# Scaling half of three layer normalizations on ScalarE, and three moves of work around it

## The chip, the core and the metric

The kernel runs on one core of one Trainium2 chip. The metric is the device time of one execution, in microseconds (us). PE is the matrix engine (TensorE), DVE is VectorE, ACT is ScalarE, POOL is GpSimd, and SP issues most of the transfers. The five run their own instruction streams and meet at semaphores.

## What is computed

Two transformer-like layers on a token array `x` of 2048 tokens by 128 features, all in float32 accuracy:

```
x = x + attention(layernorm(x))            # 16 heads with a decay
x = x + experts(layernorm(x))              # 160 experts, top 8, and a shared one
x = x + memory(layernorm(x))               # a 128x128 matrix, updated chunk by chunk
x = x + experts2(layernorm(x))             # 8 experts, top 2
layernorm(x) = (x - mean(x)) / sqrt(var(x) + 1e-5)     # over the 128 features
```

## The kernel before

The 2048 tokens lie as 16 tiles of 128 tokens (partitions) by 128 features. Four tiles are a group, and there are four groups, which I count from one in the text and the code counts from zero (`g`). Each engine's program is written out by hand, in the order in which it executes; nothing is scheduled by a tool.

There are four normalizations, `norm(0)` to `norm(3)`. The change touches the last three. I call the stretches around them stage A (`norm(1)`, ahead of the 160 experts, about 318 to 355 us), stage B (`norm(2)`, ahead of the memory, 798 to 818 us) and stage C (`norm(3)`, ahead of the 8 experts, 889 to 918 us). In each of them a group goes through five steps, one after the other:

1. DVE adds the result of the block before to `x`, takes the statistics of four tiles (L1686) and aggregates them into mean and variance (L1689).
2. POOL computes `rstd`, that is (variance + eps) to the power -0.5, in two small instructions (L685, L686).
3. DVE writes `xn`, which is (x - mean) times rstd, in four instructions (L1698). On DVE this step of a group stands behind the statistics of the next group.
4. PE transposes the four tiles of `xn` into a PSUM bank (L1175).
5. ACT copies the bank to `xnT` (L874), on which the matrix products of the block work.

What follows a group's copy differs:

- Stage A: PE does the shared expert's first product (L1307), then the router's logits (L1292), then adds biases to a later group's bank (L1286) once that bank has been read. ACT copies the shared product and takes its sigmoid (L1015, L1016), then takes the sigmoid of the logits into `gates` (L1009), then writes `xh`, a rounded copy of `xnT` (L882). DVE picks the top eight experts of each token (L1808 to L1818, L1822). When the last shared activation is there, PE clears its accumulators (L1266), and then transposes the chosen weights (L1447, L1448), which ACT scales (L1043) and copies (L1029, L1030, L1035). With these the loop over the experts begins, at 355 us.
- Stage B: PE makes two rows of token scalars per group (L1533), then sums of `xn` by chunk (L1523, L1541). PE is kept busy by products that nobody reads, called spares (L1185). DVE prepares weights and sums for these (L1968, L1978), and ACT applies a sigmoid (L887), for which it loads a table.
- Stage C: DVE first adds the memory's result to all of `x`, four instructions (L2046), and then normalizes. PE makes the router's logits (L1589), and has spares between the groups (L1172), then goes on to the up projections of the second experts (L1464), and at last spreads the chosen weights (L1617) that DVE computes from the logits (L2058 to L2094). ACT writes `xh` and POOL writes `xl` (L856), the two parts of `xnT` that the up projections read.

## Time and profile before

| | us |
|---|---|
| median of 3 runs | 1058.62 |
| lowest and highest of them | 1057.59, 1058.99 |
| the profiled execution, its time | 1059.15 |
| the profiled execution, its span in the trace | 1057.4 |
| PE busy | 1008.4 (95%) |
| DVE busy | 816.8 (77%) |
| ACT busy | 795.7 (75%) |
| POOL busy | 233.0 (22%) |

The profile shows the profiled execution alone. A row of its timeline gives the start of an instruction or of a run of equal ones (x4), counted from the start of the span, its length, the engine and the source line, and in brackets how long the engine was idle ahead of it and what ended that. The mean granted clock of PE over the span is 0.987 of full speed.

### The profile page before, as it was taken

Reading aid. Unit: us, or ns where it says so; the run is one execution under the profiler, and the core shown is the slowest. Engines: PE = TensorE matmul, PEld = TensorE weight load, DVE = VectorE, ACT = ScalarE, POOL = GpSimd, SP = SyncE. Lnnn points to the kernel's source line nnn. Section 1 sums busy time; section 2 is a strip of 40 time slices with the busy share of each in tenths; the row PEclk is TensorE's granted clock in tenths of the full one; section 3 lists DMA queues with packets and bytes.
Section 4 is the critical chain, followed back from the end, with each engine's and each line's share of the span. In section 5 each row is a group of like instructions: output and inputs, shape, how many; then the busy total and the mean of one; then the engine's idle time right before and its main releaser. Section 6 shows DMA issues by size and latency. Waiting matters only on the chain.

```text
span 1057.4 us, 20303 instructions
## 1 busy us (share of the span) xinstructions
PE 1008.4 (95%) x5242; PEld 684.2 (65%) x5274; DVE 816.8 (77%) x1861; ACT 795.7 (75%) x1331; POOL 233.0 (22%) x359
## 2 busy tenths in 40 slices
PE   5799999999998999999999999999998998999997
PEld 3333333333335688888888888888875887888885
DVE  8644444444449799999999999999996888699997
ACT  5799999999985778788787878778773553655554
POOL 3777765554463000000000000000005112200000
PEclk9799999999999999999999999999999999899999
DMA  4477876777761587677776777777631000034321
GB/s 134 143 230 242 255 250 219 235 225 226 225 202 36 180 309 246 240 243 235 240 241 241 246 245 236 235 245 242 237 98 60 1 2 1 1 128 125 106 102 40
DMA packets 102991, 188.98 MB, mean 179 GB/s; under 512 B 11932, under 2 KB 56604, under 8 KB 102940
## 3 DMA queue, kind: packets, MB, share of 16 engines
q1 hardware_dynamic: 102756, 188.19, 54.8%
q8 instruction: 18, 0.29, 0.1%
q10 hardware_dynamic: 192, 0.30, 0.1%
q14 instruction: 25, 0.20, 0.1%
HBM read 152.46 MB, written 35.98 MB: 178 GB/s over the span
## 4 chain that ended last, share of the span: by engine, by line
PE 86%; DVE 5%; ACT 3%; DMA 2%; issue 2%; POOL 1%; SPq 1%; DVEq 0%; ACTq 0%; POOLq 0%
PE bank L1464 28%; PE bank L1477 16%; PE bank L1362 12%; PE bank L1471 8%; PE bank L1343 6%; PE bank L1346 5%; PE bank L1562 1%; PE bank L1373 1%; DVE xn L1698 1%; PE bank L1185 1%; DVE stats L1686 1%; DVE state L2036 1%; DMA c_rows<-fold 1%; PE bank L1572 1%; PE bank L1292 1%
## 5 line engine op out<-in xcount | busy, mean ns | idle before, releaser
L1464 PE MATMUL bank<-xh,w_parts 128*128 128x512 f32 x896 | 277.4, 391 | 0.9 <-DVEq L1936 0.9
L969 ACT ACTIVATE ring<-bank,minus_bound 128x1024 f32<-128x1024 f32 x256 | 263.0, 1118 | 13.8 <-PE bank L1346 8.8
L1069 ACT ACTIVATE bank<-bank 128x512 f32<-128x512 f32 x320 | 186.2, 582 | 88.7 <-PE bank L1464 88.7
L1950 DVE TENSOR_TENSOR bank<-bank,ring 128x512 f32<-128x512 f32 x320 | 223.8, 699 | 25.2 <-DMA ring<-c_rows 2.8
L1477 PE MATMUL bank<-hh,w_parts 128*128 128x512 f32 x772 | 237.9, 389 | 0.0
L1942 DVE TENSOR_TENSOR hl<-bank,hh 128x512 fp32r<-128x512 f32 x321 | 218.4, 680 | 0.1
L1842 DVE TENSOR_TENSOR bank<-bank,corner 128x128 f32<-128x128 f32 x256 | 76.4, 298 | 154.3 <-PE bank L1346 151.2
L1464 PEld LDWEIGHTS bank<-xh,w_parts 128*128 128x128 f32 x896 | 168.0, 189 | 37.5 <-DVEq L1936 1.7
L1063 ACT ACTIVATE hh<-bank 128x512 fp32r<-128x512 f32 x321 | 190.4, 593 | 0.8 <-DVE bank L1950 0.5
L1464 PE MATMUL bank<-xl,w_parts 128*128 128x512 f32 x448 | 174.8, 390 | 0.0
L1477 PEld LDWEIGHTS bank<-hh,w_parts 128*128 128x128 f32 x772 | 144.8, 188 | 30.6 <-ACT hh L1063 0.8
L1471 PE MATMUL bank<-hl,w_parts 128*128 128x512 f32 x387 | 151.8, 392 | 2.5 <-DVE hl L1942 2.3
L1362 PE MATMUL bank<-ring,v_cur 128*32 128x512 f32 x1024 | 137.6, 610 | 0.1
L1343 PEld LDWEIGHTS bank<-q_stack,k_stack 128*128 128x128 bf16 x320 | 30.5, 98 | 115.8 <-ACT ring L969 96.3
L832 POOL MEMSET q_stack<- 128x512 f32 x2 | 1.0, 530 | 466.2 <-PE bank L1471 466.2
L1343 PE MATMUL bank<-q_stack,k_stack 128*128 128x384 bf16 (+2 forms) x320 | 97.7, 322 | 1.8 <-issue 0.2
L1346 PE MATMUL bank<-q_stack,k_stack 128*128 128x512 bf16 (+3 forms) x352 | 94.0, 327 | 4.2 <-DMA k_stack<-k_parts 4.2
L1464 PEld LDWEIGHTS bank<-xl,w_parts 128*128 128x128 f32 x448 | 84.4, 188 | 17.8
L1471 PEld LDWEIGHTS bank<-hl,w_parts 128*128 128x128 f32 x387 | 72.6, 188 | 22.3 <-DVE hl L1942 6.1
L1146 ACT ACTIVATE q_stack<-bank 128x512 f32<-128x512 f32 x58 | 34.7, 598 | 51.7 <-PE bank L1464 49.8
L2111 DVE TENSOR_TENSOR q_stack<-big,ring 128x512 f32<-128x512 f32 x64 | 44.3, 693 | 11.4 <-ACTq L1126 3.0
L1362 PEld LDWEIGHTS bank<-ring,v_cur 128*32 128x32 f32 x1024 | 20.2, 108 | 48.6 <-ACT ring L969 39.9
(320 smaller groups left out, 1137.7 us busy)
## 6 DMA issues: line engine op xcount, KB each, us to landing
ring<-c_rows SPq DMA_DIRECT2D x173, 512.0 KB, 4.7
w_parts<-w_pairs SPq DMA_DIRECT2D x160, 128.0 KB, 2.9
w_pairs<-xh SPq DMA_DIRECT2D x16, 768.0 KB, 4.3
q_stack<-q_parts SPq DMA_DIRECT2D x63, 144.0 KB
k_stack<-k_parts SPq DMA_DIRECT2D x189, 48.0 KB
w_pairs<-xl SPq DMA_DIRECT2D x16, 512.0 KB, 3.0
big<-in_w_exp SPq DMA_DIRECT2D x16, 384.0 KB, 4.8
w_ffn_parts<-xl SPq DMA_DIRECT2D x16, 384.0 KB, 3.7
```

Of the source, the lines that this page charges most:

```text
L969: act.activation(ring[:, c % RING * S:(c % RING + 1) * S], wide[(m + c) % SB][:], ACT.Exp, bias=minus_bound[:]).then_inc(exp_done, 1)
L1063: act.activation(hh[(c - 1) % 2][:], hidden, ACT.Copy).then_inc(split, 1)
L1069: act.activation(bank(4 + c % ZB), bank(4 + c % ZB), ACT.Silu).then_inc(silu_ready, 1)
L1343: ins = pe.matmul(wide[(m + c) % SB][:, lo:mid], k_stack[0][u][:, keys], q_stack[1][u][:, lo:mid], start=True, stop=True)
L1346: ins = pe.matmul(wide[(m + c) % SB][:, mid:hi], k_stack[1][u][:, keys], q_stack[0][u][:, mid:hi], start=True, stop=True)
L1362: ins = pe.matmul(bank(6 + u)[at:at + 32, :], v_cur[u][:, done_step % QT, :], ring[:, at_ring + h * 512:at_ring + (h + 1) * 512], start=(d ...
L1464: ins = pe.matmul(out_, w[i], x_[j], start=start and k == 0, stop=stop and k == 2, skip_group_check=not start)
L1471: return pe.matmul(bank(done_step % G), w[0], hl[done_step % 2][:], start=False, stop=False, skip_group_check=True)
L1477: ins = pe.matmul(bank(done_step % G), part, hh[done_step % 2][:], start=opens and k == 0, stop=False, skip_group_check=True)
L1842: dve.tensor_tensor(tile, tile, corner[:], ALU.mult).then_inc(corner_done, 1)
L1942: dve.tensor_tensor(hl[(c - 1) % 2][:], hidden, hh[(c - 1) % 2][:].bitcast(F32), ALU.subtract).then_inc(split, 1)
L1950: dve.tensor_tensor(bank(4 + c % ZB), bank(4 + c % ZB), cb[u][:, g * GW:(g + 1) * GW], ALU.mult).then_inc(hid_ready, 1)
```

## The change

In `norm(1)` to `norm(3)` groups two and four are no longer scaled by DVE but by ACT. ACT's instruction multiplies by one value per token and adds one per token, so POOL makes a second one, `shift` = -mean times rstd, in two more small instructions for each such group. A new semaphore, `odd_ready`, tells PE that ACT has done a group. On ACT a group's four scaling instructions stand ahead of the copy of the group before it.

In stage A PE makes a group's logits ahead of its shared product, ACT takes them in the same order, and DVE's first small product for the shared expert stands behind the first group's choice. In stage B the table for the sigmoid is loaded ahead of the normalization. In stage C DVE adds the memory's result of a group just ahead of that group's statistics, and PE's spares are three behind each group's transposes, into a bank of their own, with the group's logits right behind them.

```diff
@@ POOL
+                    if k and g % 2:
+                        link.sign(pool.tensor_scalar(shift[:, ts], mv[:, ts, 0], -1.0, None, ALU.mult))
                     link(pool.tensor_scalar(rstd[:, ts], mv[:, ts, 1], EPS, None, ALU.add))
-                    pool.tensor_tensor(rstd[:, ts], rstd[:, ts], half[:, ts], ALU.pow).then_inc(rstd_ready, 1)
+                    ins = pool.tensor_tensor(rstd[:, ts], rstd[:, ts], half[:, ts], ALU.pow)
+                    if k and g % 2:
+                        link(ins)
+                        ins = pool.tensor_tensor(shift[:, ts], shift[:, ts], rstd[:, ts], ALU.mult)
+                    ins.then_inc(rstd_ready, 1)
@@ ACT, norm(k, follow)
-                for g in range(G):
-                    n = G * k + g
-                    act.wait_ge(xnT_psum, n + 1)
-                    cols = slice(g * GW, (g + 1) * GW)
-                    act.activation(xnT[:, cols], bank(n % 2), ACT.Copy).then_inc(xnT_ready, 1)
-                    if g:
-                        follow(g - 1)
+                for g in range(G + 1):
+                    if g < G and g % 2:
+                        act.wait_ge(rstd_ready, G * k + g + 1)
+                        for t in range(g * TPG, (g + 1) * TPG):
+                            ins = act.activation(xn[:, t, :], x[:, t, :], ACT.Identity, bias=shift[:, t:t + 1], scale=rstd[:, t:t + 1])
+                        ins.then_inc(odd_ready, 1)
+                    if g >= 1:
+                        n = G * k + g - 1
+                        act.wait_ge(xnT_psum, n + 1)
+                        cols = slice((g - 1) * GW, g * GW)
+                        act.activation(xnT[:, cols], bank(n % 2), ACT.Copy).then_inc(xnT_ready, 1)
+                    if g >= 2:
+                        follow(g - 2)
@@ ACT, take_group(g)
+                take_logits(g)
                 act.wait_ge(shared_psum, g + 1)
...
-                take_logits(g)
                 high_x(g, 1)
@@ ACT, ahead of norm(2)
+            act.activation(early_table[:], half[:, 0:1], ACT.Sigmoid)
             norm(2, token_gates)
@@ PE, norm(k, read_group, spares)
-                    for _ in range(spares if g else 0):
-                        pe.matmul(bank(n % 2), hh[0][:, 0:P], hh[0][:], start=True, stop=True)
-                    pe.wait_ge(xn_ready, n + 1)
+                    if k == 0:
+                        pe.wait_ge(xn_ready, g + 1)
+                    elif g % 2:
+                        pe.wait_ge(odd_ready, G // 2 * (k - 1) + g // 2 + 1)
+                    else:
+                        pe.wait_ge(xn_ready, G + G // 2 * (k - 1) + g // 2 + 1)
...
-                    if read_group and g:
+                    if spares:
+                        for _ in range(spares):
+                            pe.matmul(bank(7), hh[0][:, 0:P], hh[0][:], start=True, stop=True)
+                        read_group(g)
+                    elif read_group and g:
                         read_group(g - 1)
@@ PE, tokens_of(g)
+                    router_logits(g)
                     shared_hidden(g)
-                    router_logits(g)
@@ PE
-            norm(3, router_logits2, 4)
+            norm(3, router_logits2, 3)
@@ DVE, norm(k, make_x)
-                    if g >= 1:
+                    if g >= 1 and (k == 0 or g % 2):
@@ DVE, choose_experts
-                shared_product(0)
                 for g in range(G):
+                    if g == 1:
+                        shared_product(0)
@@ DVE, ahead of norm(3)
-            for g in range(G):
+            def add_memory(g):
...
-            norm(3)
+            norm(3, add_memory)
```

Two places in the order of instructions matter most. The first is ACT in stage A, from the first copy on. `big` is where the gates go, `k_stack` and `q_stack` hold the shared product and its sigmoid, and L1043 is the scaling of the chosen weights. Before:

```order
L874 ACTIVATE xnT<-bank 128x512 x2
L1015 ACTIVATE k_stack<-bank 64x512
L1016 ACTIVATE q_stack<-bank 64x512
L1009 ACTIVATE big<-bank 128x640
L882 ACTIVATE xh<-xnT 128x512
L874 ACTIVATE xnT<-bank 128x512
L1015 ACTIVATE k_stack<-bank 64x512
L1016 ACTIVATE q_stack<-bank 64x512
L1009 ACTIVATE big<-bank 128x640
L882 ACTIVATE xh<-xnT 128x512
```

The same place of the changed kernel:

```order
L882 ACTIVATE xn<-x,shift,rstd 128x128 x4
L888 ACTIVATE xnT<-bank 128x512 x2
L1022 ACTIVATE big<-bank 128x640
L1029 ACTIVATE k_stack<-bank 64x512
L1030 ACTIVATE q_stack<-bank 64x512
L896 ACTIVATE xh<-xnT 128x512
L882 ACTIVATE xn<-x,shift,rstd 128x128 x4
L888 ACTIVATE xnT<-bank 128x512
L1022 ACTIVATE big<-bank 128x640
L1029 ACTIVATE k_stack<-bank 64x512
L1030 ACTIVATE q_stack<-bank 64x512
```

The scaling of group two has come ahead of the first copy, that of group four ahead of the copy of group three and behind all of group one's work, and each group's gates are ahead of its shared product.

The second is PE in stage C. `w_gate` are the logits, `hh` the spares, `ident,xn` the transposes, and the last row is the first up projection. Before, from the second group's transposes on:

```order
L1175 MATMUL bank<-ident,xn 128x128 x4
L1589 MATMUL bank<-w_gate,xnT 128x8 x4
L1172 MATMUL bank<-hh 128x512 x4
L1175 MATMUL bank<-ident,xn 128x128 x4
L1589 MATMUL bank<-w_gate,xnT 128x8 x4
L1172 MATMUL bank<-hh 128x512 x4
L1175 MATMUL bank<-ident,xn 128x128 x4
L1589 MATMUL bank<-w_gate,xnT 128x8 x8
L1464 MATMUL bank<-xh,w_parts 128x512 x2
```

The changed kernel, from the second group's transposes on:

```order
L1192 MATMUL bank<-ident,xn 128x128 x4
L1196 MATMUL bank<-hh 128x512 x3
L1610 MATMUL bank<-w_gate,xnT 128x8 x4
L1192 MATMUL bank<-ident,xn 128x128 x4
L1196 MATMUL bank<-hh 128x512 x3
L1610 MATMUL bank<-w_gate,xnT 128x8 x4
L1192 MATMUL bank<-ident,xn 128x128 x4
L1196 MATMUL bank<-hh 128x512 x3
L1610 MATMUL bank<-w_gate,xnT 128x8 x4
L1485 MATMUL bank<-xh,w_parts 128x512 x2
```

The logits of a group used to stand behind the transposes of the next one. Now they stand behind its own, with three spares between, so one group's logits are left behind the last transposes where there were two.

## Rows read from the trace of the kernel before

**Rows 1.** The page, chain that ended last, shares by engine.

```profile
PE 86%; DVE 5%; ACT 3%; DMA 2%; issue 2%; POOL 1%; SPq 1%; DVEq 0%; ACTq 0%; POOLq 0%
```

**Rows 2.** Windows of 2 us, stage A: length, PE busy, granted clock, DMA.

```profile
328.00:330.00 2.00, 2.00 (x8) 0.50 0.00 0
```

**Rows 3.** Timeline, PE, stage A: start, us, line, operands, idle before.

```profile
326.21 0.66 PE L1175 MATMUL bank<-ident,xn 128*128 128x128 f32 x4 [2.34 <-DVE xn L1698]
...
336.00 0.60 PE L1175 MATMUL bank<-ident,xn 128*128 128x128 f32 x4
...
338.82 1.07 PE L1307 MATMUL bank<-xnT,w_shared 128*64 128x512 f32 x2
...
341.16 1.19 PE L1266 MATMUL bank<-hh 128*128 128x512 f32 x4
...
346.38 0.30 PE L1447 MATMUL bank<-ident,ring 128*128 128x128 f32 x1 [0.72 <-issue]
```

**Rows 4.** Timeline, ACT, stage A.

```profile
340.52 0.58 ACT L1016 ACTIVATE k_stack<-bank 64x512 f32<-64x512 f32 x1
...
342.33 2.65 ACT L1043 ACTIVATE ring<-ring,top_inv 128x160 f32<-128x160 f32 x8
```

**Rows 5.** Timeline, DVE, stage A, and the PE row that takes its last result.

```profile
325.04 1.11 DVE L1698 TENSOR_SCALAR xn<-x,mv,rstd 128x128 f32<-128x128 f32 x4
...
326.07 0.68 DVE L1792 TENSOR_TENSOR x<-x,bank 128x512 f32<-128x512 f32 x1
...
328.04 1.11 DVE L1698 TENSOR_SCALAR xn<-x,mv,rstd 128x128 f32<-128x128 f32 x4
...
346.97 0.83 DVE L1822 TENSOR_TENSOR ring<-ring,top_inv 128x640 f32<-128x640 f32 x1
...
350.83 0.33 PE L1447 MATMUL bank<-ident,ring 128*128 128x128 f32 x1 [0.25 <-ACT fold L1030]
```

**Rows 6.** Timeline, POOL, stage A.

```profile
322.15 0.32 POOL L685 TENSOR_SCALAR rstd<-mv 128x4 f32<-128x4 f32 x1 [0.23 <-DVE mv L1689]
...
322.55 1.04 POOL L686 TENSOR_TENSOR rstd<-rstd,half 128x4 f32<-128x4 f32 x1
```

**Rows 7.** Lines, ACT, stage A: busy us, mean ns of one, idle before.

```profile
L1043 ACT ACTIVATE ring<-ring,top_inv 128x160 f32<-128x160 f32 x12 | 4.0, 414 | 0.0
```

**Rows 8.** Timeline, PE and POOL, stage B.

```profile
809.87 0.63 PE L1175 MATMUL bank<-ident,xn 128*128 128x128 f32 x4 [1.02 <-DVE xn L1698]
...
811.85 0.66 PE L1175 MATMUL bank<-ident,xn 128*128 128x128 f32 x4
...
818.35 0.63 PE L1541 MATMUL bank<-tok_sum,ident 2*128 2x32 f32 x4
...
808.73 0.31 POOL L685 TENSOR_SCALAR rstd<-mv 128x4 f32<-128x4 f32 x1 [1.57 <-DVE mv L1689]
```

**Rows 9.** Timeline, DVE and POOL, stage C.

```profile
889.31 2.48 DVE L2046 TENSOR_TENSOR x<-x,bank 128x512 f32<-128x512 f32 x4 [0.81 <-PE bank L1580]
...
900.75 3.01 DVE L1698 TENSOR_SCALAR xn<-x,mv,rstd 128x128 f32<-128x128 f32 x4 [0.54 <-POOL rstd L686]
...
900.62 1.28 POOL L856 TENSOR_TENSOR xl<-xnT,xh 128x512 fp32r<-128x512 f32 x1
```

**Rows 10.** Timeline, PE, stage C.

```profile
900.76 0.96 PE L1589 MATMUL bank<-w_gate,xnT 128*128 128x8 f32 x8
...
904.45 3.42 PE L1589 MATMUL bank<-w_gate,xnT 128*128 128x8 f32 x16
...
907.72 1.20 PE L1464 MATMUL bank<-xh,w_parts 128*128 128x512 f32 x2
...
911.15 0.39 PE L1464 MATMUL bank<-xl,w_parts 128*128 128x512 f32 x1
...
918.03 3.73 PE L1617 MATMUL bank<-ident,combine 128*128 128x128 f32 x32
```

**Rows 11.** Windows of 1 us, PE, stage C.

```profile
905.00:906.00 1.00, 1.00 (x6) 0.50 0.00 0
```

More of the change, by code:

```diff
@@ L113, in build @@
         ident = sb("ident", [P, P])
+        shift = sb("shift", [P, NT])
         half = sb("half", [P, NT])
@@ L304, in build @@
         xn_ready = sem("xn_ready")
+        odd_ready = sem("odd_ready")
         xnT_psum = sem("xnT_psum")
@@ L1176, in norm @@
                     ins.then_inc(xnT_psum, 1)
-                    if read_group and g:
+                    if spares:
[3 more added lines that the diff above has]
+                    elif read_group and g:
                         read_group(g - 1)
-                if read_group:
+                if read_group and not spares:
                     read_group(G - 1)
@@ L1312, in tokens_of @@
                     pe.wait_ge(xnT_ready, G + g + 1)
+                    router_logits(g)
                     shared_hidden(g)
-                    router_logits(g)
+                    if g < G - 2:
+                        pe.wait_ge(gate_ready, g + 1)
+                        router_biases(g + 2)
                 norm(1, tokens_of)
```

3 lines of the change are left out of this document (removed).

## The prediction

> **What bounds the kernel now.** I read the page first, then the chain that ended last, then the three stretches around the changed normalizations engine by engine in the timeline, and last the granted clock there. PE holds 86% of the chain [rows 1], and that is the loops over heads, experts and chunks, which the change leaves alone. Whatever it gives or takes, it does in stages A, B and C, 70 us together. In each of them the question is which engine's work ends last, since DVE, which loses work here, need not be that engine.
>
> Stage A. PE transposes group two at 326.21 after 2.34 us of waiting for `xn` [rows 3]. It then runs without a long gap to the last group's shared product at 338.82. ACT's last shared sigmoid starts at 340.52 and takes 0.58 [rows 4]. PE's clearing at 341.16 waits for it, and from there PE goes through nine more products and a branch to the first transposes of chosen weights at 346.38 [rows 3]. ACT copies them and is busy up to the expert loop at 355. DVE's choice of experts ends at 346.97 + 0.83 = 347.8, and PE takes it at 350.83, after a wait for ACT's copy and not for DVE [rows 5]. So DVE has 3.0 us to spare there. What bounds stage A is the way to the last shared sigmoid. In the middle of it PE has half its clock: 0.50 is granted in 328 to 330 [rows 2], that is 1.2 of 2.4 GHz, after the wait of 2.34 us.
>
> Stage B. PE waits for DVE once more at 809.87, for group three, transposes group four at 811.85, and then works through to the sums at 818.35 [rows 8]. Group four's transposes carry the rest with them.
>
> Stage C. DVE adds for 2.48 us before it takes the first statistics. Its scaling of group four takes 3.01 where the others take 1.11, while POOL's `xl` runs from 900.62 on [rows 9, 5]. PE stands idle, loses half its clock (0.50 granted at 905 to 906 [rows 11]), makes the last 16 logits instructions in 3.42 us where 8 took 0.96 at the full clock, starts the up projections at 907.72 and the spreading at 918.03 [rows 10]. Of the 36 products of the up projections 28 come from 911.15 to about 917.6, 0.23 us each, and the first eight took 907.72 to 911.15, 0.43 each [rows 10].
>
> The Trainium skill (page "SBUF — State Buffer", section "SBUF: two separate sides") has DVE and GpSimd take one shared pair of ports as a lock for a whole instruction, and ScalarE never wait for it. By that rule the 1.9 us of DVE's long scaling go away when ACT does it; the trace agrees so far as the two instructions lie side by side.
>
> **What the change costs and gives, part by part.**
>
> POOL. An odd group (two and four) gets two more small instructions. `shift` goes ahead and costs about 0.3, by the 0.32 of L685; the product behind the power costs 0.2 to 0.3 and a wait for it. A group takes from 322.15 to 323.6 [rows 6]; it will take 2.0 instead of 1.45.
>
> ACT's price for one tile is not in the trace. The nearest is L1043, one value per token, 160 columns: eight of them in 2.65, or 0.33 each when they overlap [rows 4], and 0.414 for one alone [rows 7]. Four cost 1.3 at the low end and 1.66 laid end to end. I take 1.6 since a second value per token is read. DVE's four cost 1.03 from start to next start, 325.04 to 326.07 [rows 5]. So a scaling is dearer on ACT, and what it may gain is place.
>
> The Trainium skill (page "ScalarE: Activation LUTs", section "What ACT_TABLE_LOAD costs") gives 186 ns and 0.833 ns per column, 93 ns more for each value per token, and 93 ns of overlap. By that page four would cost an estimated 1.64. The sum would be the same by it as by the upper end above.
>
> DVE. A group's turn is 3.00 from 325.04 to 328.04 [rows 5], of which 1.97 are left for an odd group.
>
> Stage A, with these. Group two: POOL is done at 322.15 + 2.0 = 324.1, ACT at 325.5 to 325.8, against 326.15 before (325.04 + 1.11). PE begins its transposes 0.4 to 0.7 earlier. Group one's gates come next, now ahead of its shared product, and are ready near 329, not 331.5. But on ACT the scaling of group four stands behind all of group one's shared work and ahead of the copy of group three. I followed the four queues with the durations of the trace, and leave the half clock where it was. ACT comes free at 331.9, scales until 333.4, copies group three until 333.9 and gives the gates of group two at 334.5. PE transposes group four at 335.0, which is 1.0 ahead of 336.00 [rows 3]. Then the new order takes it back. Before, the way from there to the end of the last sigmoid was 341.10 - 336.00 = 5.1 us. Now the last shared product stands behind the last logits, a step of 1.3, and it ends at 341.4. That is +0.3 at the dear price of ACT, and -0.6 in the expert loop's start at the cheap one; with the full clock all along it is +0.45 and -0.1. I take 0.0, bounds -0.6 and +0.6. DVE's choice begins 2 us earlier and ends 1 to 2 us earlier, which only adds to its spare time.
>
> Stage B. POOL began on group four at 808.73 [rows 8]; with one scaling less ahead of it (1.03) it begins at 807.7. POOL is done 2.0 later, with the latency at 809.6, and ACT at 811.3, with group four's transposes behind it, against 811.85 [rows 8]. -0.5, and -0.8 by the cheap ACT. Group three comes 1.0 earlier but PE has to wait for four all the same. The table load moves from a place where nobody waited to another; 0.
>
> Stage C. The first statistics begin 1.8 earlier, since three of the four adds come behind them; group four's end at 889.3 + 4 x 1.97 + 1.03 = 898.2, POOL is done at 900.2, ACT's scaling at 902.2 to 903.1, against 903.76 before (900.75 + 3.01). PE's last transposes come at 902.3 to 904, and behind them stand three spares and one group's logits instead of two. The logits are all there at 906.1 with the full clock, against 907.87. The up projections then take 36 x 0.23 = 8.3 and can't use it all, since ACT must load two tables before it takes the first banks (a new wait of 1 us for PE). The spreading starts at 916.4: -1.6. But PE now waits at group one's logits for a copy that stands behind group two's scaling, from 895.9 to 897.5. If that brings half the clock for one stretch, the same path gives 918.06: 0.0. Three of four parts to the first: -1.2.
>
> The sum is 0.0 - 0.5 - 1.2 = -1.7 on the profiled execution's 1059.15 (its span of 1057.4 and 1.75 around it), 1057.4. The profiled execution is 0.5 above the median of 1058.62 and above all three runs shown, as the place of its half-clock stretches can make it. Against the median the forecast is -1.2, or -0.1%. Less than 0.2%, 2.1 us, can hardly be told from no change here.
>
> **The rivals.**
>
> *The clock stays full* (faster). If PE's waits are short enough in A and C, the half-clock stretches go. Before they cost 1.7 in A (the same queues followed at the full clock bring ACT's last copy to 353.1, not 354.9). In C the spreading comes at 915.3 to 916.4. For it: PE's waits in A and C get shorter in sum, and the first in A shrinks from 2.34. Against it: it shrinks by only 0.5, and the spares are no more than before. -1.7 -0.5 -2.7 = -4.9: 1054.2.
>
> *ACT in PE's way* (slower). In C each copy that PE waits for is queued on ACT behind a scaling, with group one's logits at once behind. If PE's clock is halved already near 898 and again later, logits, transposes and spares up to 906 run at double length and the spreading comes at 921, +3.1. With 0.0 in A and no gain in B, it is 1062.2. It decides when PE idles for over 3 us in all between 895 and 901. For it: PE no longer has a group's transposes to do while it waits. Against it: the three spares are then just ahead of the wait.
>
> *Nothing arrives* (same). A gains nothing by its order, B's sums wait for POOL's second root, which is 0.5 later in its queue than without `shift`, and C falls to the second of its two cases: 1058.7 to 1059.8.
>
> **How the numbers follow.** Forecast 0.50, between 1056.5 and 1058.7; nothing arrives 0.17; the full clock 0.22; ACT in the way 0.11. The forecast's own bounds are A -0.6 to +0.6, B -0.8 to -0.3, C -1.6 to 0. The range of 1054.6 to 1060.6 reaches over the middle of the fast rival and up to near the slow one. Faster by over 0.2% is 0.22, slower 0.11, and the rest, 0.67, is within it.
>
> **What would show it.** ACT's four scalings take 1.3 to 1.7 from the first to the last. In A the gates of group one are taken near 329, group four is transposed near 335.0, and the last shared sigmoid still ends near 341.4; DVE's choice ends by 346.5 and PE still takes it after ACT. In B group four's transposes start 0.5 earlier against the stage's first add than before. In C no scaling of DVE is longer than 1.2, and the spreading comes 1.6 earlier than before, counted from the memory's first add at 889.31. The clock's rows tell which case has come. Wrong would be the forecast if ACT's scaling took over 2 us, if an added table load stood before it, or if the half-clock stretches move to other places than in the trace of before.

## The result

| | kernel before | changed kernel |
|---|---|---|
| median of 20 runs each, alternating on one chip | 1058.32 | 1061.78 |
| lowest and highest of them | 1053.09, 1061.79 | 1057.66, 1065.76 |
| the profiled execution, its span | 1057.4 | 1059.1 |
| mean granted TensorE clock over that span | 0.987 | 0.984 |

The ratio is 1.0034 with a 95% interval of 1.0023 to 1.0045: slower, by 3.6 us. The forecast was 1057.4, range 1054.6 to 1060.6, so the time is outside the range and on the side that had a chance of 0.11.

PE's share of the chain that ended last went from 86% [rows 1] to 87%:

```profile
PE 87%; DVE 4%; ACT 3%; DMA 2%; issue 1%; POOL 1%; SPq 1%; DVEq 0%; ACTq 0%; POOLq 0%
```

**Stage C of the changed kernel.** PE's timeline (start, length, engine, line, operands, idle ahead), from the first group's transposes to the first up projection:

```profile
894.34 0.61 PE L1192 MATMUL bank<-ident,xn 128*128 128x128 f32 x4
894.71 0.96 PE L1196 MATMUL bank<-hh 128*128 128x512 f32 x3
897.57 1.06 PE L1610 MATMUL bank<-w_gate,xnT 128*128 128x8 f32 x8 [1.90 <-ACT xnT L888]
898.48 0.64 PE L1192 MATMUL bank<-ident,xn 128*128 128x128 f32 x4
898.87 1.33 PE L1196 MATMUL bank<-hh 128*128 128x512 f32 x3
900.00 1.71 PE L1610 MATMUL bank<-w_gate,xnT 128*128 128x8 f32 x8
...
905.29 1.09 PE L1192 MATMUL bank<-ident,xn 128*128 128x128 f32 x4
906.04 1.63 PE L1196 MATMUL bank<-hh 128*128 128x512 f32 x3
907.46 1.71 PE L1610 MATMUL bank<-w_gate,xnT 128*128 128x8 f32 x8
909.03 1.20 PE L1485 MATMUL bank<-xh,w_parts 128*128 128x512 f32 x2
```

ACT and DVE over the same stretch:

```profile
895.39 1.65 ACT L882 ACTIVATE xn<-x,shift,rstd 128x128 f32<-128x128 f32 x4 [7.48 <-POOL shift L693]
896.94 0.57 ACT L888 ACTIVATE xnT<-bank 128x512 f32<-128x512 f32 x1
...
900.37 1.65 ACT L882 ACTIVATE xn<-x,shift,rstd 128x128 f32<-128x128 f32 x4
...
889.10 0.69 DVE L2069 TENSOR_TENSOR x<-x,bank 128x512 f32<-128x512 f32 x1 [0.81 <-PE bank L1601]
...
898.04 1.12 DVE L1719 TENSOR_SCALAR xn<-x,mv,rstd 128x128 f32<-128x128 f32 x4
```

Windows of the same stage (length, PE busy, granted clock):

```profile
894.00:898.00 4.00, 2.10 (x14) 1.00 0.00 0
...
902.00:907.00 5.00, 5.00 (x21) 0.50 0.00 0
907.00:912.00 5.00, 5.00 (x17) 0.50 0.00 0
912.00:913.00 1.00, 1.00 (x4) 0.56 0.00 0
```

What the edit was drawn to do on DVE and ACT, it does. No scaling of DVE is longer than 1.12, where group four's took 3.01 [rows 9], and ACT's four take 1.65. ACT is done with group four at 902.02, 12.9 us after the first addition, against 14.45 before (900.75 + 3.01 - 889.31). But PE reaches group four's transposes only at 905.29, 16.2 after that addition, where before it was 14.5. It did not wait for ACT there; the work ahead of those transposes ran at half the clock. Eight logits take 1.06 at 897.57 and 1.71 from 900.00 on. The clock is 0.50 until 912, so the first nine of the 36 up projections run at half clock too. Over the stage 6.83 us of clock are lost (the sum of one less the granted clock over windows of 1 us), before 3.42. That the half-clock stretches move to other places was one of the prediction's own signs of being wrong.

**Stages A and B.** Times in brackets are counted from the stage's first addition on DVE. In A, group two is transposed at (8.08), before (8.14); group four at (17.10), before (17.93); and the clearing stands at (23.24), before (23.09). The expert loop starts at (36.27), before (37.02); 0.72 of that is the gap named "issue" of [rows 3], which the changed kernel's two traces don't have. In B the sums come at (20.00) with one half-clock stretch, before (19.89) without. The loop's first coefficients come by DMA, and DVE waits for them:

```profile
355.50 0.70 DVE L1972 TENSOR_TENSOR bank<-bank,ring 128x512 f32<-128x512 f32 x1 [2.21 <-DMA ring<-c_rows]
...
365.50 0.70 DVE L1972 TENSOR_TENSOR bank<-bank,ring 128x512 f32<-128x512 f32 x1 [2.33 <-DMA ring<-c_rows]
```

Before, these waits were 1.84 and 0.93. The expert loop starts with the first up projection on PE. From there to stage B's first addition it is 445.4 us, before 443.4.

### The profile page after: what moved, and what is told of

The parts are those of the page before. It is cut to its first block, busy times and chain, and to the rows that moved or that the text cites. A ratio compares the mean times of both kernels' runs of the same rounds, so it can differ in the third digit from the quotient of the medians.

```text
span 1059.1 us, 20346 instructions
## 1 busy us (share of the span) xinstructions
PE 1011.8 (96%) x5274; PEld 686.9 (65%) x5274; DVE 807.4 (76%) x1837; ACT 804.4 (76%) x1356; POOL 236.0 (22%) x371
## 4 chain that ended last, share of the span: by engine, by line
PE 87%; DVE 4%; ACT 3%; DMA 2%; issue 1%; POOL 1%; SPq 1%; DVEq 0%; ACTq 0%; POOLq 0%
PE bank L1485 28%; PE bank L1498 16%; PE bank L1383 12%; PE bank L1492 8%; PE bank L1367 6%; PE bank L1364 6%; PE bank L1583 1%; PE bank L1394 1%; PE bank L1206 1%; DVE state L2058 1%; DMA c_rows<-fold 1%; PE bank L1192 1%; PE bank L1593 1%; ACT xn L882 1%; DMA ring<-c_rows 1%
## 5 line engine op out<-in xcount | busy, mean ns | idle before, releaser
L983 ACT ACTIVATE ring<-bank,minus_bound 128x1024 f32<-128x1024 f32 x256 | 262.5, 1122 | 11.8 <-PE bank L1367 6.6
L1972 DVE TENSOR_TENSOR bank<-bank,ring 128x512 f32<-128x512 f32 x320 | 223.9, 700 | 27.1 <-DMA ring<-c_rows 4.5
L1367 PE MATMUL bank<-q_stack,k_stack 128*128 128x512 bf16 (+3 forms) x384 | 98.7, 330 | 3.7 <-DMA k_stack<-k_parts 3.6
L1485 PEld LDWEIGHTS bank<-xl,w_parts 128*128 128x128 f32 x448 | 84.5, 189 | 17.7
L2133 DVE TENSOR_TENSOR q_stack<-big,ring 128x512 f32<-128x512 f32 x64 | 44.3, 692 | 11.3 <-ACTq L1140 2.9
```

The source lines that it names most:

```text
L983: act.activation(ring[:, c % RING * S:(c % RING + 1) * S], wide[(m + c) % SB][:], ACT.Exp, bias=minus_bound[:]).then_inc(exp_done, 1)
L1367: ins = pe.matmul(wide[(m + c) % SB][:, mid:hi], k_stack[1][u][:, keys], q_stack[0][u][:, mid:hi], start=True, stop=True)
L1485: ins = pe.matmul(out_, w[i], x_[j], start=start and k == 0, stop=stop and k == 2, skip_group_check=not start)
L1972: dve.tensor_tensor(bank(4 + c % ZB), bank(4 + c % ZB), cb[u][:, g * GW:(g + 1) * GW], ALU.mult).then_inc(hid_ready, 1)
```

## How the experiments are read

A single trace turned out to be a weak witness here. Which stretches have half the clock differs between two executions of one kernel, and the time with it: the kernel before ran from 1052 to 1062 us. So each kernel ran 12 times (the changed kernel a second time, as after_again, 6 times), with runs of the kernel before beside it, and with each run comes its mean granted clock. The **clock lost** of a run is its span times one less that clock. Over 384 runs of all kernels, each counted from its own kernel's mean, a microsecond of lost clock goes with 0.56 us of time (correlation 0.81). This slope is taken within kernels; where it is used below to turn a difference between two kernels into time, the result is an estimate. The mean loss of a kernel is thus a second measurement beside its time. Drawing again from the runs at random (a bootstrap) gives the difference of two such means an interval of about 2 us to each side, so that the differences of 5 to 6 below are clear, those of 2 to 3 just so or not, and those under 2 are not.

The runs beside one another were on one chip, but the batches of experiments were on four different ones, and the median of the kernel before went from 1056.75 to 1058.32 between batches. The changed kernel itself came out at 1.0034 in one batch and 1.0064 in another. So a kernel is best compared with the kernel before beside it, and differences of 1 us between kernels of different batches say little. Three single runs of two experiments (c_old_order 1068 and 2536 us, all_old_order_more 1666 us) are left out of the means of the clock. The ratio of c_old_order still has the run of 1068 us in it; the mean of its ten others is 1056.7, against 1058.0 for the kernel before beside it, which is 0.9988.

| run | median us | ratio to before (95%) | clock lost, mean us | the same of before, beside it |
|---|---|---|---|---|
| the changed kernel | 1061.78 | 1.0034 (1.0023, 1.0045) | 17.5 | |
| after_again | 1062.23 | 1.0064 (1.0040, 1.0087) | 17.7 | 11.3 |
| only_a | 1058.04 | 1.0018 (1.0003, 1.0032) | 11.6 | 11.3 |
| only_b | 1056.82 | 0.9999 (0.9984, 1.0014) | 10.2 | 11.3 |
| only_c | 1060.11 | 1.0038 (1.0019, 1.0058) | 17.7 | 11.3 |
| adds_only | 1057.74 | 0.9992 (0.9978, 1.0005) | 12.2 | 12.6 |
| c_dve | 1059.25 | 1.0008 (0.9994, 1.0022) | 16.0 | 12.6 |
| c_filled | 1058.12 | 1.0003 (0.9990, 1.0016) | 10.4 | 12.6 |
| c_old_order | 1056.55 | 1.0001 (0.9978, 1.0025) | 11.6 | 12.6 |
| new_order_only | 1059.79 | 1.0027 (1.0008, 1.0046) | 17.0 | 11.4 |
| c_four_spares | 1058.91 | 1.0018 (0.9998, 1.0038) | 13.1 | 11.4 |
| b_and_c_old_order | 1056.20 | 0.9988 (0.9972, 1.0003) | 11.6 | 11.4 |
| a_scalings_only | 1057.96 | 1.0007 (0.9989, 1.0024) | 12.2 | 11.4 |
| old_order_three | 1058.29 | 1.0017 (1.0000, 1.0033) | 14.4 | 11.8 |
| new_order_four | 1058.56 | 1.0011 (0.9997, 1.0026) | 12.2 | 11.8 |
| b_and_c_more_spares | 1055.76 | 0.9989 (0.9974, 1.0003) | 11.0 | 11.8 |
| a_logits_only | 1056.58 | 0.9990 (0.9975, 1.0006) | 11.3 | 11.8 |
| logits_b_and_c | 1054.16 | 0.9961 (0.9946, 0.9977) | 8.4 | 12.0 |
| all_old_order_more | 1057.40 | 0.9993 (0.9978, 1.0008) | 10.8 | 12.0 |

"The stage's time" below is what the traces show from the stage's first addition on DVE; in stage C up to the spreading, which is 28.7 us before and 30.5 in the changed kernel.

## The experiments

**Which stage.** Each takes one stage's part of the change alone into the kernel before (ACT's scalings, and what else of the change stands in that stage; the cut below shows the scalings alone), and the last is the changed kernel once more. In code, the changed kernel's `if k and g % 2` becomes:

```diff
+ON_ACT = (1,)      # only_a; (2,) in only_b, (3,) in only_c
-                    if k and g % 2:
+                    if k in ON_ACT and g % 2:
```

> The part of stage A alone (ACT scales groups two and four there, logits ahead of the shared product; the rest as before). Theory 1, that the loss is made in stage C by ACT's scaling in PE's way and by half-clock stretches: within 1 us of before, as the last shared sigmoid ends 0.1 to 0.3 later only. Rival, that stage A loses by the order on ACT and by transfers at the start of the expert loop: +1.5 to +3 us.

> The part of stage B alone (ACT scales there, table loaded ahead). Theory 1: -0.5 to +0.7 us, the latter where a half-clock stretch falls on the token scalars. Rival: all three stages lose about alike, +1 us or more here.

> The part of stage C alone (adds between the statistics, ACT scales, three spares and a group's own logits behind each group's transposes). Theory 1: nearly the whole loss, +2.5 to +4 us, with half clock granted for 6 us or more between 897 and 914. Rival: within 1 us of before.

> The changed kernel once more beside its parts, for a second trace and for the sum. All theories: +2.4 to +4.8 us. If the parts are independent, the three others add up to this within 1.5 us.

Stage C's part alone gives the whole loss of clock, 17.7 against 11.3 us, and a ratio of 1.0038. Stage A's part costs something too, 1.0018, with the clock lost about the same; stage B's none. The three parts add up to 3.4 us of median, and after_again measured 5.0 over the kernel before beside it, just above what was expected of it. It ran only six times, and the changed kernel's first 20 runs stood 3.5 above theirs. The changed kernel's stage C came out alike three times: the spreading at 30.5, 30.7 and, with C's part alone, 30.5, each time with 6.83 lost.

**Which part of stage C.** My theory was that ACT's scaling ahead of the copy made the 1.90 us wait, and the wait halved the clock. Four runs took it apart. Each cut shows what matters of the edit.

```diff
@@ adds_only: the kernel before, and only this
-            for g in range(G):
+            def add_memory(g):
-            norm(3)
+            norm(3, add_memory)
@@ c_dve: the changed kernel, and this
+ON_ACT = (1, 2)
@@ c_filled: the changed kernel, and this
-                        for _ in range(spares):
+                        for _ in range(spares[g]):
-            norm(3, router_logits2, 3)
+            norm(3, router_logits2, (11, 6, 6, 6))
@@ c_old_order: the changed kernel, and this
-                        for _ in range(spares):
-                            pe.matmul(bank(7), hh[0][:, 0:P], hh[0][:], start=True, stop=True)
-                        read_group(g)
+                    for _ in range(spares if g else 0):        # ahead of the transposes, as before
+                        pe.matmul(bank(n % 2), hh[0][:, 0:P], hh[0][:], start=True, stop=True)
...
+                    if read_group and g:
+                        read_group(g - 1)
-            norm(3, router_logits2, 3)
+            norm(3, router_logits2, 4)
```

> The kernel before with one part of the change alone: in stage C the three later additions of the memory stand between the statistics; DVE keeps all four scalings and PE its old order. Theory 1 (the loss of stage C comes from ACT's scalings and PE's new order, not from the additions): the statistics of the first group come 1.8 us earlier, and at worst the same half-clock stretch stays, so the spreading is due at 27.0 to 28.7 us from the stage's first addition (28.7 before) and the time is 0 to 1.6 us under the kernel before. Theory 2 (the additions between the statistics hold DVE up for the later groups and so open the gaps on PE): the spreading comes at 29.5 or later, with more than 3.4 us of clock lost in the stage, and the time is at or above the kernel before.

> The changed kernel with one thing undone: in stage C DVE scales groups two and four again, with the additions between the statistics and PE's new order as in the changed kernel. Theory 1 (ACT's scaling of group two stands ahead of its copy of group one, PE waits 1.9 us for that copy and then has half its clock): without the scaling on ACT PE's copy of group one comes near 5.2 + 0.7 us in the stage instead of 8.3, no wait of over 1 us is there, 3.4 us of clock or less is lost in stage C, and the spreading is due by 28.7; 1.5 to 2 us under the changed kernel. Theory 2 (the loss is PE's new order, with the transposes of the next group no longer ahead of the logits, so that PE has nothing to do while it waits for DVE and POOL): the clock lost stays near 6.8 us and the spreading at 30 or later; within 0.5 us of the changed kernel.

> The changed kernel with more of PE's spare products in stage C: 11, 6, 6 and 6 behind the four groups' transposes instead of 3 each, nothing else. Theory 1 (the loss in stage C is the half clock that follows PE's waits): the spares lie in the waits, the clock stays at 2.4 GHz for all or nearly all of the stage (lost 0 to 1.7 us against 6.8), and the spreading is due at 26 to 28 us from the first addition against 30.5; 2 to 4 us under the changed kernel, so at or under the kernel before. Theory 2 (the loss is the queue on ACT itself, the copies behind the scalings and table loads): the clock may be full, but the spreading still comes at 30 or later and the time is that of the changed kernel or above it.

> The changed kernel with PE's old order in the normalizations: four spares ahead of each group's transposes in stage C, and a group's logits behind the transposes of the next group; ACT still scales groups two and four. Theory 1 (ACT's scaling ahead of the copies is the cause): the last transposes still wait for ACT, PE's gaps are as long as in the changed kernel, the clock lost stays at 5 us or more and the spreading at 29.5 or later; within 1 us of the changed kernel. Theory 2 (PE's new order is the cause): clock lost 3.4 us or less, the spreading by 28.7, 1.5 us or more under the changed kernel.

The additions are harmless, and by themselves worth nothing: with the full clock throughout the spreading stands at 27.2 in adds_only, and at 27.1 in only_b, whose stage C is that of the kernel before. With ACT's scalings undone in C (c_dve) the 1.90 us wait is gone, as theory 1 said, and yet the clock is lost all the same: 6.82 in the trace, 16.0 in the mean of the runs. PE's timeline and windows of c_dve:

```profile
896.45 1.06 PE L1609 MATMUL bank<-w_gate,xnT 128*128 128x8 f32 x8
898.04 0.66 PE L1191 MATMUL bank<-ident,xn 128*128 128x128 f32 x4 [0.54 <-DVE xn L1718]
898.46 0.95 PE L1195 MATMUL bank<-hh 128*128 128x512 f32 x3
899.39 1.35 PE L1609 MATMUL bank<-w_gate,xnT 128*128 128x8 f32 x8
901.14 1.08 PE L1191 MATMUL bank<-ident,xn 128*128 128x128 f32 x4 [0.40 <-DVE xn L1718]
...
895.00:899.00 4.00, 3.46 (x23) 1.00 0.00 0
...
901.00:912.00 11.00, 10.86 (x38) 0.50 0.00 0
```

Ahead of the fall PE waited 0.54 us, and the half clock came. In the kernel before it waited 1.09 and 0.62 there and had the full clock until the third wait. So the theory that the wait for ACT's copy takes the clock falls. The time did not go by theory 2 alone, though: c_dve's median is 1059.25, 2.5 under the changed kernel, where theory 2 had them within 0.5, and its spreading came 0.7 earlier (29.8). With PE's new order ACT's scalings in C thus seem to cost some time beside the clock; only_c and new_order_only, which differ by the scalings and the additions, are only 0.3 us of median apart, so this stays open.

The run with ACT's scalings and PE's old order settles what loses the clock: 11.6 us lost, 5.9 fewer than in the changed kernel, and a median of 1056.55 beside 1057.94 of the kernel before. In its trace the spreading is at 25.7. A single trace says little here, too: a later version, b_and_c_old_order, has the same instructions in stage C, lost 6.82 us there in its trace and spread at 29.9; over its 12 runs it, too, lost 11.6. PE in c_old_order, then in b_and_c_old_order, from the second group's transposes on:

```profile
896.29 0.66 PE L1193 MATMUL bank<-ident,xn 128*128 128x128 f32 x4 [1.19 <-ACT xn L883]
...
901.26 0.66 PE L1193 MATMUL bank<-ident,xn 128*128 128x128 f32 x4 [0.16 <-ACT xn L883]
901.75 2.04 PE L1607 MATMUL bank<-w_gate,xnT 128*128 128x8 f32 x16
```

```profile
894.15 0.65 PE L1193 MATMUL bank<-ident,xn 128*128 128x128 f32 x4 [1.19 <-ACT xn L883]
...
901.06 1.05 PE L1193 MATMUL bank<-ident,xn 128*128 128x128 f32 x4
901.91 3.42 PE L1607 MATMUL bank<-w_gate,xnT 128*128 128x8 f32 x16
```

The extra spares (c_filled) take the loss away too, 10.4, and the spreading stands at 27.7 without any half clock: 2 us later than with the old order; with 29 spares where there were 12, PE transposes group four at (14.74) and not at (12.96).

**The order, or the number of spares.** The new order has one spare fewer at each group, though 12 in all as before (four times three, not three times four).

```diff
@@ new_order_only, new_order_four: the kernel before, and this, with 3 or 4
-                    for _ in range(spares if g else 0):
-                        pe.matmul(bank(n % 2), hh[0][:, 0:P], hh[0][:], start=True, stop=True)
...
-                    if read_group and g:
-                        read_group(g - 1)
+                    for _ in range(spares):
+                        pe.matmul(bank(7), hh[0][:, 0:P], hh[0][:], start=True, stop=True)
+                    read_group(g)
@@ c_four_spares: the changed kernel, and this
-            norm(3, router_logits2, 3)
+            norm(3, router_logits2, (4, 4, 4, 4))
@@ old_order_three: the kernel before, and this
-            norm(3, router_logits2, 4)
+            norm(3, router_logits2, 3)
```

> The kernel before with one thing alone: PE's new order in stage C (three spares behind each group's transposes and then that group's own logits, instead of four spares ahead of the transposes of groups two to four and the logits of the group before behind them). DVE keeps all scalings, the additions all stand ahead. Theory 1 (the order is what costs the clock in stage C, as the run with the order undone and the one with ACT's scalings undone suggest): the half clock begins within a few us of the first logits and holds to the up projections, 5 to 7 us of clock are lost in the stage, the spreading comes 2 to 4 us later than in the kernel before, and the time is 1.5 to 3.5 us over it. Theory 2 (the order costs only together with the additions between or with ACT's scalings): clock lost in stage C 3.4 us or less, the spreading at 27 to 28.8, within 1 us of the kernel before.

> The changed kernel with four spare products behind each group's transposes in stage C instead of three, nothing else. Theory 1 (the place of the spares and of the logits decides, not the one spare): the clock is lost as in the changed kernel, 5 us or more in stage C, and the spreading stands at 30 or later; time within 1 us of it. Theory 2 (the one spare fewer per group is what tips it): clock lost 3.4 us or less, the spreading at 26.5 to 28.5, and 2 us or more under the changed kernel.

> The kernel before with three spares ahead of the transposes of groups two to four in stage C instead of four, so 9 in all instead of 12, and nothing else. Over the runs of a kernel the clock lost (span times one less the granted clock) has been 10.6 to 12.7 us in the middle for the kernel before and 16 to 18 with PE's new order and three spares. Theory 1 (the number of spares near each group is what tips it): 15 us or more lost in the mean of the runs, and 1.5 to 3 us over the kernel before. Theory 2 (the place is what tips it: logits, wait and transposes in a row without the next group's transposes between them): 11 to 13 us lost and within 1 us of the kernel before.

> PE's new order alone, as in an earlier run, but with four spares behind each group's transposes instead of three, 16 in all. Theory 1 (the number of spares near each group): 11 to 13 us of clock lost in the mean of the runs, against 17.0 with three, and within 1 us of the kernel before. Theory 2 (the place): 16 us or more lost and 2 to 3 us over the kernel before.

The new order with three spares, and nothing else of the change, loses 5.6 us of clock more than the kernel before and is at 1.0027. A fourth spare takes nearly all of that back: 12.2 against 11.8 lost. In the changed kernel it takes most of it, 13.1 against 17.5. And three spares in the old order lose 2.6 more than four. So the number counts: a fourth spare is worth 2.6 us of clock in the old place and 4.8 in the new one. The place counts with three spares, 2.6 in the old place against 5.6 in the new one, which the 12 runs of each barely tell apart, and hardly with four (none against 0.4). In time the same four kernels stand at 1.0017, 1.0027, 1.0011 and, for the kernel before, 1, with intervals that overlap, so the ranking rests on the clock. Three things go together in the new place and were not separated: the spares stand behind the transposes and not ahead of them, the group's own logits stand between them and the next wait, and they write another bank. The trace of new_order_only shows where, the rows that answer to [rows 10]:

```profile
903.28 1.09 PE L1190 MATMUL bank<-ident,xn 128*128 128x128 f32 x4 [1.23 <-DVE xn L1717]
904.02 1.63 PE L1194 MATMUL bank<-hh 128*128 128x512 f32 x3
905.44 1.71 PE L1608 MATMUL bank<-w_gate,xnT 128*128 128x8 f32 x8
907.01 1.20 PE L1483 MATMUL bank<-xh,w_parts 128*128 128x512 f32 x2
...
900.00:902.00 2.00, 2.00 (x14) 1.00 0.00 0
902.00:904.00 2.00, 0.77 (x5) 0.52 0.00 0
```

Here the clock falls in the wait for group four. With only one group's logits behind group four's transposes, the up projections start at 907.01, 18.4 after the first addition, as before; the half clock then stays for more of them and the spreading comes at 29.6. c_four_spares shows how little one trace says: its own had 5.12 us lost in stage C and the spreading at 31.1, later than any other, while its 12 runs lost 4.4 us less than the changed kernel. Its median lies between the two kernels, as neither theory had it.

**Stage A's two halves, and a faster version.**

```diff
@@ a_scalings_only: the kernel before, and ACT's scalings in norm(1)
+ON_ACT = (1,)
@@ a_logits_only: the kernel before, and the logits first on PE, ACT and DVE (ACT's part shown)
+                take_logits(g)
                 act.wait_ge(shared_psum, g + 1)
...
-                take_logits(g)
@@ b_and_c_old_order: scalings in B and C, additions between, stage A as before
+ON_ACT = (2, 3)
+            norm(3, add_memory)
@@ b_and_c_more_spares: the same, and spares (0, 7, 4, 5) in the old place
@@ logits_b_and_c: the same, and the logits first in stage A
@@ all_old_order_more: the same, and ON_ACT = (1, 2, 3)
```

> The kernel before with the scalings of groups two and four on ACT in stages B and C, and the additions between the statistics, but PE's old order in stage C and nothing changed in stage A. Theory 1 (stage C gains once PE keeps its old order, and stage A's part of the change costs 1 to 2 us up to stage B by whatever cause): the spreading at 25.7 to 26.5 from the stage's first addition, B's sums 0.2 to 0.5 earlier, and 2 to 3 us under the kernel before: the fastest of all. Theory 2 (stage A's part costs nothing): the same time as the changed kernel with the old order in C alone, within 0.7 us.

> The kernel before with one thing alone: ACT scales groups two and four in stage A, in front of its copies of groups one and three, while the logits stay behind the shared product. Theory 1 (the shift of the last shared product behind the last logits is what stage A pays): the transposes come as early as in the changed kernel, the clearing 1 us before it, at 22.2 or so from the stage's first addition, and the time is at or 0.5 to 1 us under the kernel before. Theory 2 (ACT's scalings ahead of the copies are what it pays): the transposes of group four no earlier than in the kernel before, the clearing at 23.1 or later and the time at or 1 to 2 us above the kernel before.

> The run with the scalings on ACT in stages B and C, the additions between and PE's old order, nothing of stage A, which measured 1056.20 and lost 11.6 us of clock in the mean; now with 7, 4 and 5 spares ahead of the transposes of groups two, three and four instead of 4 each. If the clock in stage C hangs on the spares, 8 to 10 us are lost in the mean and the time is 1 to 2 us under that run, 2 to 3 under the kernel before. If the added spares delay the transposes as much as the clock gives back, it is the same as that run.

> The kernel before with one thing alone: in stage A the router's logits stand ahead of the shared product on PE, ACT and DVE, and DVE keeps all scalings. Theory 1 (this order is what makes stage A dearer, by the last shared product behind the last logits): the clearing 0.5 to 1 us later than in the kernel before with the same clock, and 0.5 to 1.5 us over it. Theory 2 (ACT's scalings are): no later than the kernel before, within 0.5 us of it. Beside that, the seventh product with the experts' coefficients on DVE starts 10.2 to 11.3 us after the first up projection in the kernels with the old stage A, and 11.3 to 13.4 in those with the new one; where it stands at 12 or more here, the order of the logits is tied to it, and where at 11.3 or less, it is not.

> The version with ACT's scalings in stages B and C, the additions between, PE's old order and 7, 4 and 5 spares, plus the logits ahead of the shared product in stage A; DVE keeps the scalings of stage A. If the parts add up (that version measured 0.9989 and the logits alone 0.999), this one comes at 0.998, 1.5 to 3 us under the kernel before, the first to be faster than it beyond doubt. If the two gains were each chance, it is within 1 us of the kernel before.

> The changed kernel with one thing undone, PE's order in stage C (four spares ahead of the transposes and the logits a group later), and with 7, 4 and 5 spares; so the version beside it plus ACT's scalings in stage A. If ACT's scalings in stage A cost 0.5 to 1 us, as the runs of A's halves suggest (1.0007 with them alone, 0.999 with the logits alone), this is 0.5 to 1.5 us over the version beside it, and 3 to 5 us under the changed kernel with 10 to 12 us of clock lost. If they cost nothing, the two are equal within 0.5 us.

ACT's scalings are what stage A pays, by most of these runs. logits_b_and_c and all_old_order_more differ by them alone, and stand at 0.9961 and 0.9993: 3.2 us of median (by a bootstrap of the means 1.7 to 4.7), of which an estimated 1.3 is clock (2.4 more lost, at 0.56). That is more than the 0.5 to 1.5 that was expected. Alone they cost 1.0 (a_scalings_only). Two other kernels that differ by the whole of stage A's part, c_old_order and b_and_c_old_order, are within 0.4 us, as theory 2 of the latter had it, so the size is uncertain. The traces show the place. In the changed kernel ACT scales group four ahead of group three's copy and group two's gates, and PE waits for those gates (ACT first, then PE):

```profile
330.43 1.64 ACT L882 ACTIVATE xn<-x,shift,rstd 128x128 f32<-128x128 f32 x4
331.96 0.58 ACT L888 ACTIVATE xnT<-bank 128x512 f32<-128x512 f32 x1
332.44 0.69 ACT L1022 ACTIVATE big<-bank 128x640 f32<-128x640 f32 x1
...
333.18 0.57 PE L1307 MATMUL bank<-bias_rows,ones_r 128*128 128x320 f32 x2 [1.11 <-ACT big L1022]
333.59 0.60 PE L1192 MATMUL bank<-ident,xn 128*128 128x128 f32 x4
```

With the logits first and DVE scaling (a_logits_only) PE has no wait between its rows there:

```profile
329.59 1.07 PE L1321 MATMUL bank<-xnT,w_shared 128*64 128x512 f32 x2
330.59 0.56 PE L1303 MATMUL bank<-bias_rows,ones_r 128*128 128x320 f32 x2
330.99 0.60 PE L1192 MATMUL bank<-ident,xn 128*128 128x128 f32 x4
```

Group four is transposed at (15.83) and the clearing stands at (21.97), against (17.93) and (23.09) before and (17.10) and (23.24) in the changed kernel, all with 1.70 us of clock lost in the stage. So with that loss the logits first give 1.1 us, and ACT's scalings take 1.3. With the full clock throughout stage A the clearing is at (21.51) in the old stage A (only_b) and at (21.81) in the changed one (c_old_order): 0.3 late and not 0.15.

logits_b_and_c beats both kernels: 1054.16, 0.9961 of the kernel before (0.9946 to 0.9977) and 7.6 us of median under the changed one. The gain is twice what the two parts had measured (0.9989 and 0.9990), so part of it may be chance. Its stage C, PE again:

```profile
894.14 1.84 PE L1187 MATMUL bank<-hh 128*128 128x512 f32 x7
896.52 0.66 PE L1193 MATMUL bank<-ident,xn 128*128 128x128 f32 x4 [0.53 <-ACT xn L883]
...
901.51 0.66 PE L1193 MATMUL bank<-ident,xn 128*128 128x128 f32 x4
902.00 2.04 PE L1607 MATMUL bank<-w_gate,xnT 128*128 128x8 f32 x16
...
914.20 3.73 PE L1635 MATMUL bank<-ident,combine 128*128 128x128 f32 x32
...
900.00:905.00 5.00, 5.00 (x33) 1.00 0.00 0
```

The spreading comes 25.7 us after the first addition. Of the five versions with PE's old order and ACT's scalings in C, the three with 7, 4 and 5 spares had no half clock in stage C in their traces and lost 11.0, 8.4 and 10.8 us over the whole program in the mean; the two with four each lost 1.71 and 6.82 in stage C in their traces and 11.6 in the mean. That leans to more spares, and doesn't prove them.

## Why the prediction was wrong

**Durations of the parts**: right. ACT's four scalings measured 1.65 (taken 1.6, bounds 1.3 to 1.7). The 1.64 that the prediction estimated from the Trainium skill (page "ScalarE: Activation LUTs", section "What ACT_TABLE_LOAD costs") agrees. A POOL group with `shift` takes 2.2 with the latencies between (2.0). The long scaling of DVE is gone, and in c_dve, where DVE scales group four again, it takes 1.99 beside one `xl` of POOL (901.40 to 902.68), against 3.01 beside two. That fits the rule of the Trainium skill (page "SBUF — State Buffer", section "SBUF: two separate sides"). The stage did not get shorter for it.

**Stage A, 0.0**: right as a sum (the clearing at +0.15), wrong in its parts. The prediction let ACT's scalings give the gain and wrote that the new order "takes it back". Measured it is the other way: the order alone gives 1.1, the scalings alone come to (24.23), 1.1 late with more clock lost (3.41 in the stage against 1.70), and group two's transposes come 0.06 earlier and not 0.4 to 0.7. ACT started them at (6.38), 0.3 later than drawn, and was dearer than the cheap end by as much.

**Stage B, -0.5**: right in sign, too large. Without a half-clock stretch the sums come at (19.71) to (19.74), -0.15 to -0.2. POOL begins at the predicted time, but its chain and ACT's end 0.3 later than drawn. only_b's ratio, 0.9999, has room for either.

**Stage C, -1.2**: this step failed. "Three of four parts to the first" was the first of two cases, the full clock, and the other was one stretch of half clock. Both left out what the spares do for the clock: the sum for the new order counted "three spares and one group's logits instead of two" as length only, and the sentence against the fast rival, that "the spares are no more than before", put no price on having three at each wait instead of four. With the old order the gain that the step describes is there where the clock holds: 25.7 against 28.7, -3.0, of which about 1.6 is clock (with the full clock the kernel before's stage C takes 27.1). With the new order and three spares it is +1.8.

**The rival "ACT in PE's way"** named the outcome, 1062.2, with a chance of 0.11, and had the clock halved near 898 for +3.1 in C. The changed kernel's clock fell near 899, but the mechanism was wrong, so that the number comes out near 1061.78 is mostly luck: C gave +1.8, and the rest came from elsewhere. It was to come when PE idles over 3 us between 895 and 901; PE idled 1.9 there in the changed kernel and 0.9 in c_dve between 895 and 902, and the clock fell in both. Its sentence against, "the three spares are then just ahead of the wait", was the point: three were not enough in that place. The loss of clock in C is the order with its spares (new_order_only 1.0027), and ACT's scalings in C cost nothing that shows once the order is the old one.

**The bill** is an estimate. 17.5 against some 12 us of lost clock, 5.5 at 0.56, is 3.1 of the 3.6 us. ACT's scalings in stage A take about 2 beside the clock and the logits there give about 1; stage C's additions and scalings give 1.4 at the full clock. That leaves about 1 us open, which is within what the runs can tell. A candidate is the wait for the first coefficients: from the loop's start to stage B it is 442.8 to 444.0 us in the ten traces in which at most one stage is changed, and 443.8 to 446.1 in nine of the ten others. But all_old_order_more, the tenth, has 443.2, with every part of stages A and B in it, and a_logits_only, made to test a tie to the order of the logits, starts the seventh product with the coefficients 10.9 us after the loop's start, as the old stage A does (10.2 to 11.3), so it shows none. No part of the change could be tied to it, and nothing in the traces says what delays it.

**The range** was too narrow above, since it was built on one trace's half-clock stretches, with "The clock stays full" (0.22) at twice the chance of "ACT in PE's way" (0.11). One trace can stand over 3 us from the middle of its kernel's runs (c_four_spares, span 1060.7 and so 1062.4 in all, against 1058.9).

## What to carry to other kernels

Where dummy products hold TensorE's clock over a string of waits, they are part of the schedule like any wait. Moving them, or taking one away per wait, is to be costed at half clock for a stretch of the work behind, not at the length of the products. Count the mean of the lost clock over a dozen runs (span times one less the granted clock), since one trace shows one throw. And when a change bundles several edits, cost each alone: here the harmful two (PE's order with three spares, ACT's scalings in stage A) hid a rest that by itself, with four more spares than before, made the kernel 0.4% faster in its 12 runs.

## What the runs showed of the hardware

The granted clock falls and comes back in single executions of one kernel at the same place of the program or not: b_and_c_old_order lost 6.82 us in stage C in its trace and c_old_order, with the same instructions in that stage, 1.71. Over the runs of the kernel before the loss was 5.3 to 20.1 us. Between executions of one kernel, a microsecond more of lost clock goes with 0.56 us more of time. And it was not the length of the wait ahead that told whether the clock falls: c_old_order and b_and_c_old_order both waited 1.19 us for group two, and in the second the clock fell 2 us after that wait, while in the first it held for over 7 us more; there were 0.54 us ahead of the fall in c_dve, while adds_only had waits of 1.36, 0.53 and 1.06 us in the same stage, four spares each, at the full clock throughout.
